# A fused embedding, attention and mixture-of-experts kernel: work of the first expert block placed in the attention's last steps

## The reference

```python
h = (weight[x] + (lora_A.T[x] @ lora_B.T) * 2) * magnitude * norm      # embedding; norm needs the whole 32000-row table
h = h + attention(layernorm(h))        # 16 heads of 32; all four products on quantized inputs and ternary weights
n = layernorm(h)
shared = (silu(n @ Wsg.T) * (n @ Wsu.T)) @ Wsd.T                       # 704 hidden columns
gates  = top_2(softmax(n @ Wr.T))                                      # 8 experts
routed = sum over the 2 chosen experts e: gate_e * (silu(n @ Wg[e].T) * (n @ Wu[e].T)) @ Wd[e].T   # 352 hidden columns each
out = h + routed + shared
```

## Time and profile before

| | us |
|---|---|
| median of 3 runs (1498.35 to 1503.94) | 1501.03 |
| the profiled execution | 1505.97 |
| its span, first to last instruction | 1503.9 |
| TensorE busy | 1395.4 (93%) |
| VectorE busy | 1118.7 (74%) |
| ScalarE busy | 876.5 (58%) |
| GpSimd busy | 395.9 (26%) |
| embedding | 0 to about 210 |
| attention | about 210 to 601 |
| shared blocks, routed blocks, shared blocks | 601 to 1504 |

### The profile page before, as it was taken

The page is one execution under the profiler, slowest core; times in us unless marked ns, Lnnn a source line. Parts: engine busy times, 40 slices in busy tenths (PEclk is TensorE's granted clock), DMA queues, the critical chain, the costliest instruction groups (busy, mean ns, idle before and its releaser), DMA issues.

```text
span 1503.9 us, 37424 instructions
## 1 busy us (share of the span) xinstructions
PE 1395.4 (93%) x14294; PEld 1142.1 (76%) x14294; DVE 1118.7 (74%) x2215; ACT 876.5 (58%) x1502; POOL 395.9 (26%) x494
## 2 busy tenths in 40 slices
PE   6687869999999996899999999999999999999998
PEld 1221237777777774899999999989989889999997
DVE  4477847989999985776647777877778778677776
ACT  4688946777777774423325666666566665533331
POOL 6500054445444420013211211111111110133333
PEclk8899979999999997899999999999999999999998
DMA  9999952323223211131114788777786777444365
GB/s 343 399 366 358 418 144 45 79 65 76 71 63 84 56 49 52 58 115 56 42 43 138 246 263 273 240 262 253 255 277 233 260 251 242 172 136 139 126 222 197
DMA packets 77905, 269.42 MB, mean 179 GB/s; under 512 B 9696, under 2 KB 10336, under 8 KB 71392
## 3 DMA queue, kind: packets, MB, share of 16 engines
q1 hardware_dynamic: 61360, 223.88, 41.8%
q0 software_dynamic: 16432, 44.05, 11.2%
HBM read 224.12 MB, written 43.78 MB: 178 GB/s over the span
## 4 chain that ended last, share of the span: by engine, by line
PE 38%; DVE 9%; issue 6%; ACT 4%; DMA 2%; DVEq 0%; POOL 0%; ACTq 0%; another core or an unknown queue 0%; SPq 0%; POOLq 0%
PE up_ps L1770 7%; PE up_ps L1771 7%; PE up_ps L1772 7%; PE down_ps L1771 4%; PE down_ps L1772 4%; PE down_ps L1770 4%; DVE w_split L1533 3%; ACT w_split L1448 2%; DMA w_stage<-packed 2%; DVE xT_lo L1524 2%; PE up_ps L1804 1%; DVE h L1674 1%; PE up_ps L1799 1%; DVE w_split L1534 1%; ACT h_hi L1470 1%
## 5 line engine op out<-in xcount | busy, mean ns | idle before, releaser
L1770 PE MATMUL up_ps<-xT_hi,w_split 128*128 128x256 f32 x1280 | 368.0, 287 | 16.1 <-DVE xT_lo L1524 8.3
L1772 PE MATMUL up_ps<-xT_hi,w_split 128*128 128x256 f32 x1280 | 364.3, 285 | 0.0
L1771 PE MATMUL up_ps<-xT_lo,w_split 128*128 128x256 f32 x1280 | 364.3, 285 | 0.0
L1770 PEld LDWEIGHTS up_ps<-xT_hi,w_split 128*128 128x128 f32 x1280 | 247.4, 193 | 19.1 <-issue 8.9
L1771 PEld LDWEIGHTS up_ps<-xT_lo,w_split 128*128 128x128 f32 x1280 | 247.6, 193 | 1.3
L1772 PEld LDWEIGHTS up_ps<-xT_hi,w_split 128*128 128x128 f32 x1280 | 247.5, 193 | 0.0
L1470 ACT ACTIVATE h_hi<-h 128x256 fp32r<-128x256 f32 (+1 forms) x192 | 80.2, 418 | 258.4 <-DVE h L1674 188.5
L1416 POOL DMA_INDIRECT xr<-x_rows,slot_tokens x71 | 75.4, 1062 | 420.5 <-PE xT_ps L1863 376.1
L1448 ACT ACTIVATE w_split<-w_stage 128x1408 fp32r<-128x1408 f32 (+1 forms) x123 | 169.7, 1410 | 22.9 <-DMA w_stage<-packed 19.5
L1770 PE MATMUL down_ps<-w_split,h_hi 128*128 128x512 f32 (+1 forms) x405 | 160.1, 395 | 3.4 <-DVE H L1653 3.4
L1772 PE MATMUL down_ps<-w_split,h_lo 128*128 128x512 f32 (+1 forms) x405 | 161.3, 398 | 0.0
(11 more groups left out here) (303 smaller groups left out, 2986.1 us busy)
## 6 DMA issues: line engine op xcount, KB each, us to landing
W<-table SPq DMA_DIRECT2D x48, 1280.0 KB, 9.0
w_stage<-packed SPq DMA_DIRECT2D x80, 704.0 KB
w_stage<-packed SPq DMA_DIRECT2D x40, 768.0 KB, 4.4
xr<-x_turned SPq DMA_DIRECT2D x32, 512.0 KB
slot_rows<-y_rows SPq DMA_DIRECT2D x32, 512.0 KB
x_rows<-x SPq DMA_DIRECT2D x32, 256.0 KB, 2.0
x_turned<-x2T SPq DMA_DIRECT2D x32, 256.0 KB, 3.8
out<-H SPq DMA_DIRECT2D x32, 256.0 KB
```

Source lines behind the costliest of these rows:

```text
L1770: pe.matmul(out, a_hi, b_hi, start=first, stop=False)
L1771: pe.matmul(out, a_hi, b_lo, start=False, stop=False)
L1772: return pe.matmul(out, a_lo, b_hi, start=False, stop=last)
```

## The change: what it does

1. Buffers. `FirstBlocks` holds what both stages now share: `S`, the split weights `w_split0`, the rows `xr0`, `xT_hi` and `xT_lo` of both buffers, and their semaphores. In the experts the four banks of `S` serve as `xT_ps`, the third `up_ps` bank and `route_ps`. The rows of block 1 are loaded over the two q buffers `QT` of the attention, behind their last use.
2. Weights. In the steps 21 to 27 ScalarE makes the high part of the first shared half, one piece a step (four of 704 columns, three of 512). In the steps 25 to 31 GpSimd makes the low part (four of 640, two of 2x64, three of 512).
3. Rows. SyncE loads the rows of block 0 in step 28 and those of block 1 in step 32; ScalarE and VectorE split them in the steps 30 to 33.
4. Block 0's up products, into `S`: 12 behind the turn of `outT` in step 32, 36 behind that step's output projection, 20 behind the last logits.
5. Experts. TensorE's first work there is block 1. The plan's parts come one block later, all but `plan_slots` and `mark_slots`. The rows of blocks 4 and 5 are asked for ahead of the wait for `blocks_known`.

```diff
+class FirstBlocks:
+    def __init__(self, ctx, nc):
+        self.S = ctx.enter_context(nc.psum_tensor("S", [P, GROUPS, 512], F32))
+        self.w_split = sb("w_split0", [P, 2 * PACKED], F32R)
+        self.xr = sb("xr0", [P, 2, D])
...
@@ attend, sync @@
+                for odd, seq, xr in ((0, SEQS - 7, first.xr[:, :, :]), (1, SEQS - 3, second_rows)):
+                    if isinstance(back3.i, int) and back3.i == seq:
+                        for b in range(2):
+                            sp.wait_ge(x2T_out[b], 16 * 2)
+                        if odd:
+                            sp.wait_ge(shifted_done, SEQS * GROUPS)
+                        sp.dma_start(xr, x2T_dram[odd * 2:odd * 2 + 2, :, :].rearrange("s p d -> p s d")).then_inc(first.rows_in[odd], 16)
@@ attend, gpsimd: at the end of each step @@
+            def up_lo(k):
+                pool.wait_ge(first.w_hi_done[k // 2], 1)
+                pool.tensor_tensor(first_w.up_lo[:, k, :], staged_up[:, k, 0:BOTH_FROM], first_w.up_hi[:, k, 0:BOTH_FROM].bitcast(F32),
+                                   ALU.subtract).then_inc(first.w_lo_done[k // 2], 1)
...
+            def first_lo(i):
+                if i == SEQS - 7:
+                    up_lo(0)
+                    up_lo(1)
+                elif i == SEQS - 6:
+                    narrow_lo(0)
+                elif i == SEQS - 5:
+                    up_lo(2)
+                    up_lo(3)
+                elif i == SEQS - 4:
+                    narrow_lo(1)
+                elif i == SEQS - 2:
+                    down_lo(0)
+                    down_lo(1)
+                elif i == SEQS - 1:
+                    down_lo(2)
@@ attend, scalar: first_hi(now.i) ahead of the wait for heads_done @@
+            def first_hi(i):
+                k = i - (SEQS - 11)
+                j = k - KT
+                if 0 <= k < KT:
+                    after(act, stage_in, 16)
+                    hi = act.activation(first_w.up_hi[:, k, :], staged_up[:, k, :], ACT.Copy)
...
+                elif i == SEQS - 2:
+                    first_rows_hi(0)
...
+                    if back1.i == SEQS - 1:
+                        first_rows_hi(1)
@@ attend, vector @@
+                if back1.yes and back1.i == SEQS - 1:
+                    first_rows_lo(0)
...
+                if back2.yes and back2.i == SEQS - 1:
+                    first_rows_lo(1)
@@ attend, tensor @@
                     turn(bank[2], outT).then_inc(out_turned, 1)
+                    if isinstance(back1.i, int) and back1.i == SEQS - 1:
+                        first_up_half(0, 0)
...
                     pe.matmul(bank[1][:, 0:EXPERTS], logit_parts[:, :], at_strip[:, 0:EXPERTS], start=True, stop=True).then_inc(logits_done, 1)
+                    if isinstance(back2.i, int) and back2.i == SEQS - 1:
+                        up_tail(pe, S[:, 2, :], first_w, first.xT_hi[0], first.xT_lo[0]).then_inc(first.up_done, 1)
...
                     mm.then_inc(projected, 1)
+                    if isinstance(back1.i, int) and back1.i == SEQS - 1:
+                        first_up_half(0, 1).then_inc(first.up_done, 1)
+                        first_up_half(1, 0)
+                        first_up_half(1, 1).then_inc(first.up_done, 1)
@@ experts @@
-            load_rows(0, 0, 0)
-            load_rows(1, 1, 0)
-            load_rows(2, 0, 0)
-            load_rows(3, 1, 0)
+            for n in range(2, 6):
+                load_rows(n, n % 2, 0)
             sp.wait_ge(blocks_known, 1)
             block_weights(0)
...
-            plan_choices()
-            each_block(dve, body, plan_blocks, plan_experts, plan_slots, mark_slots, None, read_table)
+            each_block(dve, body, plan_choices, plan_blocks, plan_experts, plan_slots, mark_slots, None, read_table)
...
-            each_block(pe, body, count_choices, before_twelfth=sum_table)
+            each_block(pe, body, None, count_choices, before_twelfth=sum_table)
```

More of the change, by code:

```diff
@@ L560, in attend @@
         scale_bc = sb("scale_bc", [P, T])
-        QT = pair("QT", [P, KT, T])
+        QT_all = sb("QT", [P, 2, KT, T])
+        QT = [QT_all[:, i, :, :] for i in range(2)]
         K_T = pair("K_T", [P, KT, T])
@@ L891, in project, with first_up_half, weigh @@
                 return mm
-            def weigh(seq, j, first, last):
+            def first_up_half(j, half):
+                if (j, half) == (0, 0):
+                    pe.wait_ge(exp_done, SEQS * GROUPS)
+                    pe.wait_ge(first.xT_lo_done, 1)
+                    for piece in range(2):
+                        pe.wait_ge(first.w_lo_done[piece], LO_STEPS[piece])
+                return up_tile_half(pe, S[:, j, half * BLOCK:(half + 1) * BLOCK], first_w, first.xT_hi[0], first.xT_lo[0], j * 2 * P + half * P)
+            def weigh(seq, j, begin, last):
                 for m in range(PER_GROUP):
@@ L902, in weigh @@
                     mm = pe.matmul(bank[3][to, 0:T], group_ones[:, j, :], probT[:, j, m * T:(m + 1) * T],
-                                   start=first, stop=last, skip_group_check=True)
+                                   start=begin, stop=last, skip_group_check=True)
                 return mm
@@ L1488, in body @@
             def body(n, odd, kind, kind_before, kind_after):
-                if kind_after:
+                if kind_after and not is_first(n):
                     turned_hi(n + 1, 1 - odd, kind_after)
@@ L1777, in up_full @@
                     pe.wait_ge(w_lo_done[piece], (w + 1) * LO_STEPS[piece])
-                def part(out, at, f, k, first, last):
-                    hi, lo = up_hi[buffer][:, k, at:at + f], up_lo[buffer][:, k, at:at + f]
-                    return three(out, hi, lo, xT_hi[odd][:, k, :], xT_lo[odd][:, k, :], first, last)
                 for j in range(2):
-                    after(pe, h_done, (n - 1) * 4 + j + 1)
+                    if not is_first(n, 1):
+                        after(pe, h_done, (n - 1) * 4 + j + 1)
                     for half in range(2):
-                        for k in range(KT):
-                            mm = part(up_ps[j][:, half * BLOCK:(half + 1) * BLOCK], j * 2 * P + half * P, P, k, k == 0, k == KT - 1)
+                        mm = up_tile_half(pe, up_ps[j][:, half * BLOCK:(half + 1) * BLOCK], weights[buffer], xT_hi[odd], xT_lo[odd], j * 2 * P + half * P)
                     mm.then_inc(up_done, 1)
@@ L1883, in tower @@
         w_stage = sb("w_stage", [P, PACKED])
+        with nc.sbuf_tensor("W", [P, SLOTS, CHUNK_TILES, D], F32) as W:
+            pass
+        first = FirstBlocks(ctx, nc)
         with ExitStack() as attention:
+            y = [attention.enter_context(nc.sbuf_tensor(f"y{i}", [P, D], F32)) for i in range(2)]
+            z2 = attention.enter_context(nc.sbuf_tensor("z2", [P, D], F32))
             wT = [attention.enter_context(nc.sbuf_tensor(f"wT_{n}", [P, KT, D], BF16)) for n in "qkvo"]
```

214 lines of the change are left out of this document (128 added, 86 removed).

## The result

| | before | changed |
|---|---|---|
| median of 20 runs each, us | 1504.11 | 1493.34 |
| lowest and highest | 1498.35 to 1510.47 | 1488.57 to 1502.92 |
| ratio of the two, 95% interval | | 0.9941 [0.9929, 0.9953] |
| the profiled execution, and its span | 1505.97, 1503.9 | 1491.15, 1489.4 |

The change makes the kernel 8.9 us faster by the ratio (7.1 to 10.7). Two later measurements of the same pair gave 0.9926 [0.9906, 0.9945] and 0.9932 [0.9910, 0.9954], so 10 us is a fair figure. One run of a variant (rows of blocks 4 and 5 late) took 2231.72 us at a mean granted clock of 0.56 and is left out of that variant's ratio. The profiled pair differs by 14.5 us of span.

A forecast was written before the change was run, and what follows sets the result against it. TensorE was taken to bound attention and experts, with a hole between them. 14.3 - 1.0 - 0.5 = 12.8 us off the 1501.03 median gave 1488.2, range 1483 to 1496 for 8 in 10.

The forecast's parts named there:

- The border: From attention to experts: what begins at 617.41 us begins at 603.1, 14.3 us earlier.
- The clock on the way there: Attention's end: projection at granted clock 0.50, full level back after 4.65 us of unbroken work, at about 594.6.
- rival A: Attention's end: the clock never falls, turn of the last x 2.2 us earlier, gain 15.0, 1486.0 us; chance 0.10.
- The stall at block 5: Block 5: TensorE waits once for the bank that block 4 frees, 0.8 to 1.1 us, taken as 1.0.
- The bank stall of 0.2 in block 1: Block 1: TensorE wants block 0's last bank after 5.7 us, VectorE frees it after 5.9: 0.2 lost.
- The rows and the plan: Rows of blocks 4 and 5 asked for early so the later plan doesn't hold them: worth 0 against before.
- ScalarE: Attention: seven activations of 0.7 us stand in ScalarE's 1.0 us wait of each step, cost 0.
- Rival C: Attention: ScalarE's seven activations show in full, 4.6 us, 1492.8 us; chance 0.08.
- GpSimd: Attention, steps 25 to 31: its subtractions cost VectorE's time beside them, 0 to 2.5 us, taken as 0.5.
- nothing is given back behind block 5: Routed blocks: the stall at block 5 comes once, and the sum has no further loss after it.

The follow-up runs named there:

- the best kernel: Changed kernel with GpSimd's first pair a step later, block 1's row split in VectorE's last-logits wait, 6 of the last 20 products behind the last x's turn: 0.9908.
- the kernel that had spread its products most: Changed kernel with GpSimd's first pair a step later, block 1's row split behind the last gates, the last 20 products cut 6, 3, 11: ratio 0.9927.
- the row split alone: Changed kernel with only VectorE's low part of block 1's rows moved behind the last gates: ratio 0.9913 to the kernel before.

## Why the prediction was right, and where its sizes were off

**The border: right in sum.** Forecast: what begins at 617.41 begins 14.3 us earlier, and 1.0 is given back at block 5, so 13.3. Measured: 13.7 from A to B. Block 1's up products were forecast 18.9 us behind the outT turn (602.9 less 583.96) and came at 18.98, 19.83 and 17.47.

**The clock on the way there: not as forecast.** The projection at half clock was seen in one of three traces of the changed kernel, and there the full level came back some 3 us behind the projection's start, not 4.65; rival A, the clock never falls, was whole in another. In the first and second it fell in the last 20 products, which no case had. That the sum held is partly luck. In the profiled trace the last logits began 14.1 us behind A, where 15.7 was forecast, and the 20 products behind them then ran mostly at the half level and ended at 18.5, where 18.4 was forecast: the missing fall ahead of the projection and the unforeseen one behind the logits cancel.

**The stall at block 5: right.** 1.0 forecast from VectorE's chain of 51.1 us, 0.9 measured, once, released by VectorE's h. The bank stall of 0.2 in block 1 did not show in these traces: its 68 products and their down products follow in 8.19 us.

**The rows and the plan: right.** Nothing against before, and 12 us if taken away.

**ScalarE: right.** Steps 21 to 24 and 27 take 11.16 or 11.17 us, as without the seven activations. Rival C is out.

**GpSimd: right place, wrong size.** I took 0.5 out of 0 to 2.5, since the even durations of xT_lo in the earlier trace rows seemed to say that VectorE isn't held up. It cost 1.27, all of it in step 25; the second pair cost nothing. In the row I leaned on GpSimd was the one held up; here VectorE was. The Trainium skill (SBUF — State Buffer, section "Who interferes with whom") says that the two exclude each other for a whole instruction, whoever comes first. The traces agree, in both directions: VectorE's 0.17 became 1.85, and GpSimd's 0.27 became 1.25.

**The step that failed: nothing is given back behind block 5.** The sum had no term for the routed blocks, and they take 2.5 us longer. What the traces show of it: VectorE splits the down weights when ScalarE has their high part, 40 times. In the three traces of before VectorE starts 0.03 us behind ScalarE's end; in all eleven of the changed kernel and its variants it starts 0.10 behind it (in nine of the eleven one start, 0.46 behind, is left aside). Before, then after, ScalarE's instruction and VectorE's:

```profile
897.43 1.48 ACT L1448 ACTIVATE w_split<-w_stage 128x1536 fp32r<-128x1536 f32 x1
```

```profile
898.94 1.76 DVE L1530 TENSOR_TENSOR w_split<-w_stage,w_split 128x1536 fp32r<-128x1536 f32 x1 [0.85 <-ACT w_split L1448]
```

```profile
881.54 1.48 ACT L1611 ACTIVATE w_split<-w_stage 128x1536 fp32r<-128x1536 f32 x1
```

```profile
883.13 1.76 DVE L1690 TENSOR_TENSOR w_split<-w_stage,w_split 128x1536 fp32r<-128x1536 f32 x1 [0.93 <-ACT w_split L1611]
```

897.43 + 1.48 is 898.91, and VectorE follows at 898.94. 881.54 + 1.48 is 883.02, and it follows at 883.13. Where VectorE sets the pace this adds up from block to block. In the trace of the best kernel, which lacks the 0.46, the split of the down weights stands 0.07, 0.15, 0.23, 0.30 and 0.38 us further behind TensorE's down products than in before, in five blocks in a row (counted behind the down products of blocks 19 to 23). Then, behind the second half block, TensorE waits where it didn't wait before (0.27 us), and the step from block 24 to 25 is 14.00 instead of 13.6. The first half block, ahead of C, costs nothing: B to C is the same to 0.02. Between C and D stand six half blocks. Six times 0.38 would be 2.3, near the 2.5 measured, but that is an estimate: TensorE waits behind the other five in both kernels, and those steps scatter from 14.2 to 17.3 us over the traces, so that only one of the six can be read by itself. TensorE's waits for this one releaser over the whole stage, before and after:

```profile
PE up_ps L1770 <- DVE h L1693: 7.9, 5, 2.0
```

```profile
PE up_ps L536 <- DVE h L1854: 9.8, 6, 2.1
```

Why the handover is 0.07 longer can be read from the traces. The change raised the increment that these instructions give their own semaphore from 1 to 2 or 3 (`LO_STEPS` from 2, 2, 1 to 3, 3, 3), so that GpSimd's smaller pieces could count alike. In before, the record of such a split names both semaphores, the one it waits for and the one that it raises. In the changed kernel the record names only the second, with its larger step, and the wait is a record of its own, an `EVENT_SEMAPHORE` on VectorE that starts 0.07 us ahead of the split. The kernel before has the same case in code that the change left alone. The low part of a half block's h raises its semaphore by 2 (L1705), and where it waits for ScalarE it too starts 0.10 behind ScalarE's end: six starts in the three traces, all 0.10. ScalarE's instruction and VectorE's, before:

```profile
1060.62 0.26 ACT L1486 ACTIVATE h_hi<-route_ps 96x128 fp32r<-96x128 f32 x1
```

```profile
1060.99 0.42 DVE L1705 TENSOR_TENSOR h_lo<-route_ps,h_hi 128x256 fp32r<-128x256 f32 x1 [1.61 <-ACT h_hi L1486]
```

Beside it, the low parts of whole blocks, which raise theirs by 1, start 0.03 behind in both kernels. So the larger increment costs the handover 0.07. That the handovers make the whole loss of the routed blocks is argued from one step and from the waits; no run took the increments back to 1.

**The predicted time.** 1488.2 against a median of 1493.3: inside the range of 1483 to 1496, but above the forecast's own 1485 to 1491, and nearest to the price of rival C, whose cause did not occur. Of the 5.1 us, 3.1 are the base: the three runs of before had a median of 1501.03, twenty had 1504.11. The rest is the gain itself, 12.8 forecast: 10.8 by the medians, 9.9 by the traces. By the traces 2.9 are missing: GpSimd's 0.8 and the 2.5 of the routed blocks, less the 0.4 that the border gave more.

## What to carry to other kernels

Do not stop at hiding the preparation of a piece of work; put the work itself into an engine's idle time: the hidden splits alone paid 4.2 us from A to B, the products in the attention's waits 9.5 more. When work of GpSimd is placed beside VectorE, look at who starts first, not at how long either runs: the smallest VectorE or GpSimd instruction on the path can take the length of the other's. And when a stage that you did not mean to touch shares a helper or a counter with one that you did, compare its handovers too. Here a counter that steps by 2 or 3 made each handover 0.07 us longer, on an engine that sets the pace there, and the routed blocks took back a fifth of what the change had won (2.5 of 12.4).

## What the runs showed of the hardware that was not expected

- The granted clock at one place of one kernel differs from execution to execution. In three traces of the changed kernel it fell in the last products, there and ahead of the projection, or not at all, worth 2.3 us from A to B.
- In the kernel that had spread its products most, TensorE waited 1.95 us at the barrier, and the clock fell 0.6 us later, in block 1. The spread won nothing ahead of the barrier (block 1's up products at 16.91 us behind A, with the row split alone 16.93), and A to B was 0.4 longer (76.78 against 76.34).
- The lock between VectorE and GpSimd stretches instructions of one or 16 elements a partition from 0.27 and 0.17 us to 1.25 and 1.85 us.
- A VectorE instruction that waits for ScalarE and raises its own semaphore by 2 or 3 starts 0.10 us behind ScalarE's end; one that raises it by 1 starts 0.03 behind.
